# The next item's turn behind both halves of gate and up, and the routing tables written late, in an adaLN attention and expert block on one core

## The chip, the cores and the metric

The kernel runs on one core of a Trainium2 chip. The metric is the device time of one execution in microseconds (us), lower is better. The core has five engines with an instruction stream each: TensorE (PE, with its weight loads as PEld), VectorE (DVE), ScalarE (ACT), GpSimd (POOL) and SyncE (SP). Each works through its stream in order; they meet only at semaphores, which one engine raises and another waits for.

## The reference

For 4 sequences of 512 tokens of width 256 the reference computes an adaLN block: modulation rows from a condition, attention, and a mixture of experts.

```python
h = _layernorm(x) * (1 + ca) + sa
x = x + ga * attention(h)          # 16 heads of 16, 4 key/value heads
h = _layernorm(x) * (1 + cb) + sb
probs = softmax(h @ router_w.T)    # 8 experts
w = _top_p_weights(probs, 0.9)     # keep the likeliest experts up to 0.9
for e in range(8):
    g = silu(h @ gate_w[e].T)      # 256 -> 512
    u = h @ up_w[e].T
    out = out + ((g * u) @ down_w[e].T) * w[:, e:e+1]
x = x + gb * out
```

All of it is in f32. The expert products are made of three matmuls each: an operand is rounded to a high part (ScalarE) and its rest becomes a low part (VectorE), and high times high, high times low and low times high are added.

## The kernel before, in words

**Start.** SP loads the condition, the first sequence and the weights. VectorE computes the means and variances of sequence 0 and GpSimd takes the power (L337). VectorE then writes `xhat` (L660), which TensorE turns (L1102) and projects to queries, keys and values. Meanwhile GpSimd writes constants, one after another (L339 to L353): zeros and ones, two masks (`tie`, `earlier`), `ones_b`, the ones of `v_aug`, and four tables by iota (`slot_row`, `slot_tile`, `token1`, `pad_row`). Each raises `consts`; GpSimd waits for all eight, then for the variances of sequences 1 to 3, takes their power (L357), and issues four DMAs that write zeros to `y_rows` and to the end of `h_rows`. VectorE and TensorE both wait for all of `consts` before attention. Of these constants attention reads only the ones of `v_aug`; the rest is for routing.

**Attention** runs sequence by sequence. While the scores, exponentials and products of sequence b run, the engines also prepare sequence b + 1 and finish b - 1. Then come the routing and the lists of tokens for each expert.

**Experts.** The tokens of each expert are cut into items of 256 (two tiles of 128 rows). In this input there are 25 items in all. In the loop over items each engine runs one body for item m, and the bodies are written out by hand:

- GpSimd gathers the rows of a later item into `h_sel` (L391, two indirect DMAs). It does so when the turn of the item before has read `h_sel` (`turned`) and VectorE has copied that item's weights from it (`w_copied`). It then scatters the outputs of an earlier item with addition (L404, two indirect DMAs).
- TensorE: gate and up for the first half of the hidden width (`gate_up(m, half, 0)`, L1340, 24 matmuls), the turn of item m + 1 (`turn`, L1326, 4 transposes), gate and up for the second half (24 matmuls), then down of item m - 1 in two halves (`down`, L1353, 12 matmuls each, one after the other). The next item's first matmul waits for `sel_lo`.
- ScalarE: silu of the first half (`gate`, L557); once both halves of item m are done, the high part of the next input (`round_input`, L552, writes `hs_hi`); then the high part of the first hidden half (`round_hidden`, L562, writes `a_hi`), silu of the second half, and its high part.
- VectorE: copy of the next item's weights (`take_weights`, L1014), product of the first half (`product`, L1020, writes `a_full`), low part of the next input (`split_input`, L1008, writes `hs_lo`, raises `sel_lo`), low part of the first hidden half (`split_hidden`, L1025, writes `a_lo`), product of the second half, output of item m - 1 (`output`, L1035, writes `y_sel`), low part of the second hidden half.

`hs_hi`, `hs_lo`, `h_sel` and `psM` exist once. `a_hi` and `a_lo` exist once for each half, and are read by `down`. Hence the wait in ScalarE's `round_hidden`, with `FREE = 2` and `down_ps` raised by 2 at the start and by 1 for each half of down:

```python
act.wait_ge(a_ready, 2 * m + h + 1 + FREE)
act.wait_ge(down_ps, 2 * m + h - 1 + FREE)
```

After the first item of an expert ScalarE rounds the next expert's weights and VectorE splits them (`between_experts`). The loop over experts is a loop over four pairs, and every engine jumps back three times.

Of the kernel before, what the change touches and what calls it, by code (L numbers as in the profile page):

```python
# [21 lines left out]
P = 128  # L22
# [8 lines left out]
def adaln_block(nc, x, wqT, wkT, wvT, woT, routerT, gateT, upT, downT, cT, wmod, out):  # L31
# [29 lines left out]
    with ctx:  # L61
# [14 lines left out]
        def sems(names):  # L76
            return [sem(n) for n in names.split()]
# [78 lines left out]
        for parts, part in ((w_hi, "w_hi"), (w_lo, "w_lo")):  # L156
# [43 lines left out]
        zeroed, ident_done, consts, silu_step, modc_ps, modc_done, modr_ps, row_copied, mod_out, mod_in, gate_step, modr_done = sems(  # L200
            "zeroed ident_done consts silu_step modc_ps modc_done modr_ps row_copied mod_out mod_in gate_step modr_done")
# [25 lines left out]
        NCONST = 8  # L227
# [98 lines left out]
        def _(pool):  # L326
# [11 lines left out]
            for m, v in ((v_aug[:, :, :, :, D:YROWS], 0.0), (tie[:, :, :], 1.0), (earlier[:, :], 1.0), (zeros[:, :], 0.0)):  # L338
                pool.memset(m, v).then_inc(zeroed, 1)  # L339
# [6 lines left out]
            pool.memset(v_aug[:, :, :, :, D:D + 1], 1.0).then_inc(consts, 1)  # L346
# [5 lines left out]

# [3 lines left out]
            pool.wait_ge(ln1_eps, 2)  # L356
            pool.tensor_tensor(rstd1[:, TT:], var_eps1[:, TT:], minus_half[:, 0:NT - TT], ALU.pow).then_inc(ln1_rstd, 1)  # L357

            for r0, r1 in ((0, T // 2), (T // 2, T), (T, T + PADS)):
                pool.dma_start(y_rows[r0:r1, :].rearrange("(t p) c -> p t c", p=P),  # L360
                               zeros[:, 0:C].rearrange("p (o c) -> p o c", o=1).broadcast_to([P, (r1 - r0) // P, C])
                               ).then_inc(scattered, 16)
            pool.dma_start(h_rows[T:T + PADS, :].rearrange("(t p) c -> p t c", p=P),
                           zeros[:, :].rearrange("p (o c) -> p o c", o=1).broadcast_to([P, S, ROW])).then_inc(scattered, 16)
# [66 lines left out]
        def _(act):  # L431
# [132 lines left out]
            def body(e, e2, first, m, half):  # L564
                gate(m, 0)
                act.wait_ge(up_ps, 2 * m + 2)
                round_input(m + 1)
                round_hidden(m, 0)
                gate(m, 1)
                round_hidden(m, 1)  # L570
# [17 lines left out]
        def _(dve):  # L588
# [319 lines left out]
            dve.wait_ge(consts, NCONST)  # L908
            attention(dve, body)
            take_sums(B - 1, G - 1)  # L910
            finish_y(B - 1, (B - 1) % 2, G - 1)
            choose_experts(0)
# [99 lines left out]

# [27 lines left out]
            def body(e, e2, first, m, half):  # L1040
                take_weights(m + 1)
                product(m, 0)
# [356 lines left out]
```

## Time and profile before

| | us |
|---|---|
| median of 3 runs | 614.0 (613.22 to 616.6) |
| the profiled execution, its own time | 614.37 |
| span of its profile | 612.6 |
| TensorE busy | 483.4 (79% of the span) |
| VectorE busy | 371.3 (61%) |
| ScalarE busy | 282.5 (46%) |
| GpSimd busy | 170.9 (28%) |

The span starts with the first instruction and ends with the last. Times in rows are microseconds from its start; the mean granted TensorE clock is 0.894 of full speed. The rest of the execution's own time (1.8 us) lies outside the span.

### The profile page before, as it was taken

What the parts mean: (1) busy time and instruction counts of PE and PEld (TensorE: products, weight loads), DVE (VectorE), ACT (ScalarE), POOL (GpSimd) and SP (SyncE); (2) the same over time, 40 slices, a digit from 0 to 9 for tenths busy, and PEclk for the clock granted to TensorE, in tenths of its full rate; (3) what the DMA queues carried; (4) which work ended last, traced back from release to release, by engine and by line L of the source; (5) the groups of instructions that cost most, each with busy time, mean ns of one, the idle gap of its engine ahead of it and who ended that gap; (6) DMA issues with size and microseconds to landing.
All of it is one profiled execution on the core that took longest, in us unless ns stands there. A gap on an engine that the chain in (4) does not pass through costs nothing. (4 is left out here: it accounts for less than half of the span.)

```text
span 612.6 us, 10534 instructions
## 1 busy us (share of the span) xinstructions
PE 483.4 (79%) x3498; PEld 351.2 (57%) x3499; DVE 371.3 (61%) x910; ACT 282.5 (46%) x409; POOL 170.9 (28%) x184
## 2 busy tenths in 40 slices
PE   2745978898899789997315599999997998999810
PEld 2333323244344433425215599999997998999810
DVE  4496287669936983567678175665643755465526
ACT  0244669776886788782000244453423543443300
POOL 6104000000000000000000336656665556476440
PEclk9965989998999999987655699999998998999975
DMA  8243100000000010010121134636453446333338
GB/s 291 95 135 117 61 1 1 1 0 2 24 13 1 1 35 1 1 35 1 34 73 35 46 104 98 158 60 164 90 125 61 109 98 151 56 52 60 44 37 271
DMA packets 33815, 42.01 MB, mean 69 GB/s; under 512 B 5620, under 2 KB 26868, under 8 KB 33784
## 3 DMA queue, kind: packets, MB, share of 16 engines
q0 software_dynamic: 10400, 16.22, 14.5%
q1 hardware_dynamic: 23384, 25.39, 13.0%
q8 instruction: 18, 0.29, 0.2%
q14 instruction: 13, 0.11, 0.1%
HBM read 28.14 MB, written 13.46 MB: 68 GB/s over the span
## 5 line engine op out<-in xcount | busy, mean ns | idle before, releaser
L511 ACT ACTIVATE probs<-psS 128x1024 f32<-128x1024 f32 x128 | 124.0, 1023 | 16.3 <-PE psS L1162 16.0
L1340 PE MATMUL psS<-hs_hi,w_hi 128*128 128x256 f32 x400 | 117.5, 294 | 6.9 <-issue 3.9
L1340 PE MATMUL psS<-hs_lo,w_hi 128*128 128x256 f32 x400 | 114.4, 286 | 0.0
L1340 PE MATMUL psS<-hs_hi,w_lo 128*128 128x256 f32 x400 | 114.3, 286 | 0.0
L404 POOL DMA_INDIRECT y_rows<-y_sel,idx_out x50 | 83.4, 1668 | 55.3 <-DVE y_sel L1035 45.0
L1340 PEld LDWEIGHTS psS<-hs_hi,w_hi 128*128 128x128 f32 x400 | 77.5, 194 | 8.4 <-issue 7.7
L1162 PE MATMUL psS<-qT,kT 96*128 96x512 bf16 x256 | 71.7, 393 | 11.1 <-ACT probs L511 9.4
L1340 PEld LDWEIGHTS psS<-hs_lo,w_hi 128*128 128x128 f32 x400 | 77.7, 194 | 0.0
L1340 PEld LDWEIGHTS psS<-hs_hi,w_lo 128*128 128x128 f32 x400 | 77.5, 194 | 0.0
L1271 PE MATMUL psY<-probs,v_aug 128*32 128x512 f32 x512 | 70.8, 626 | 0.0
L369 POOL TENSOR_TENSOR rstd<-var_eps,minus_half 128x4 f32<-128x4 f32 x4 | 4.8, 1195 | 235.2 <-DVE var_eps L764 235.2
L552 ACT CAST hs_hi<-psM 128x512 fp32r<-128x512 f32 x26 | 15.3, 587 | 117.0 <-PE psS L1340 76.7
L391 POOL DMA_INDIRECT h_sel<-h_rows,idx_in x50 | 52.9, 1058 | 38.6 <-issue 20.3
L1353 PE MATMUL psY<-w_hi,a_hi 128*128 128x256 f32 x200 | 56.1, 280 | 1.6 <-DVE y_sel L1035 1.6
L1353 PE MATMUL psY<-w_lo,a_hi 128*128 128x256 f32 x200 | 56.0, 280 | 0.0
L1353 PE MATMUL psY<-w_hi,a_lo 128*128 128x256 f32 x200 | 56.0, 280 | 0.0
L1008 DVE TENSOR_TENSOR hs_lo<-psM,hs_hi 128x512 fp32r<-128x512 f32 x26 | 18.0, 692 | 59.5 <-ACT hs_hi L552 51.5
L562 ACT CAST a_hi<-a_full 128x512 fp32r<-128x512 f32 x50 | 31.1, 621 | 42.7 <-PE psY L1353 23.2
L1162 PEld LDWEIGHTS psS<-qT,kT 96*128 96x128 bf16 x256 | 21.5, 99 | 46.9 <-ACT probs L511 29.9
L1025 DVE TENSOR_TENSOR a_lo<-a_full,a_hi 128x512 fp32r<-128x512 f32 x50 | 34.6, 692 | 20.1 <-ACT a_hi L562 16.1
L1353 PEld LDWEIGHTS psY<-w_hi,a_hi 128*128 128x128 f32 x200 | 37.6, 188 | 1.8 <-issue 1.8
L1353 PEld LDWEIGHTS psY<-w_hi,a_lo 128*128 128x128 f32 x200 | 37.6, 188 | 0.0
(188 smaller groups left out, 807.6 us busy)
## 6 DMA issues: line engine op xcount, KB each, us to landing
w_in<-gateT SPq DMA_DIRECT2D x8, 512.0 KB
w_in<-upT SPq DMA_DIRECT2D x8, 512.0 KB
w_in<-downT SPq DMA_DIRECT2D x8, 512.0 KB
x_all<-x SPq DMA_DIRECT2D x4, 512.0 KB, 7.9
mod_rows<-mod_table SPq DMA_DIRECT2D x4, 512.0 KB, 7.6
y_rows<-zeros POOLq DMA_DIRECT2D x2, 1024.0 KB
h_rows<-h_nat SPq DMA_DIRECT2D x4, 512.0 KB, 3.0
y_all<-y_rows SPq DMA_DIRECT2D x4, 512.0 KB, 5.7
```

Of the source, the lines that this page charges most:

```text
L369: pool.tensor_tensor(rstd[:, :], var_eps[:, :], minus_half[:, 0:TT], ALU.pow).then_inc(ln_rstd, 1)
L391: pool.indirect_dma_start(h_sel[:, k, :], None, h_rows[:, :], bass.IndirectOffsetOnAxis(ap=idx_in[:, k:k + 1], axis=0)).then_inc(gathered, 16)
L404: pool.indirect_dma_start(y_rows[:, :], bass.IndirectOffsetOnAxis(ap=idx_out[:, k:k + 1], axis=0), y_sel[:, k, :], None, compute_op=ALU.ad ...
L511: act.activation(probs[:, gk % 4, 2 * pair:2 * pair + 2, :], psS[:, pair, :, :], ACT.Exp, scale=ATT_SCALE).then_inc(probs_done, 1)
L552: act.copy(hs_hi[:, :, :].rearrange("p k t -> p (k t)"), psM[:, 0, :]).then_inc(sel_hi, 1)
L562: act.copy(a_hi[:, 2 * h:2 * h + 2, :].rearrange("p i t -> p (i t)"), a_full[:, h, :]).then_inc(a_rounded, 1)
L1008: dve.tensor_tensor(hs_lo[:, :, :].rearrange("p k t -> p (k t)"), psM[:, 0, :], hs_hi[:, :, :].rearrange("p k t -> p (k t)").bitcast(F32), ...
L1025: dve.tensor_tensor(a_lo[:, 2 * h:2 * h + 2, :].rearrange("p i t -> p (i t)"), a_full[:, h, :], a_hi[:, 2 * h:2 * h + 2, :].rearrange("p i ...
L1162: mm = pe.matmul(psS[:, u % 2, j, :], kT[:, parity, g, kt * P:(kt + 1) * P], qT[:, parity, g * R + 2 * pair + j, :], start=True, stop=True)
L1271: mm = pe.matmul(psY[r * YROWS:(r + 1) * YROWS, g % 2, :], v_aug[:, parity, kt, g, :], probs[:, gk % 4, r, :], start=kt == 0, stop=kt == T ...
L1340: mm = pe.matmul(ps[:, i * SW:(i + 1) * SW], w, v[:, k, :], start=at == 0, stop=at == 3 * KC - 1)
L1353: mm = pe.matmul(psY[:, j, 0:C], v[:, i, tok], w, start=i == 0 and n == 0, stop=i == KI - 1 and n == 2)
```

## The change

In the expert loop the turn of item m + 1 moves behind both halves of gate and up. ScalarE's body becomes: silu of the first half, high part of the first hidden half, silu of the second half, high part of the next input, high part of the second hidden half. VectorE's body becomes: product and low part of the first half, the copy of the next item's weights, product of the second half, low part of the next input, low part of the second hidden half, output of item m - 1. No wait inside these helpers changes.

At the start GpSimd writes only `v_aug` (its ones raise a semaphore of their own, `v_ones`), then waits for the variances of sequences 1 to 3, takes their power, writes `zeros` and issues the four DMAs; after them come the masks and the four tables. TensorE waits for `v_ones` before the first score, and for `consts` before the ranks; VectorE waits for `consts` before it chooses experts.

```diff
             pool.wait_ge(ln1_eps, 1)
             pool.tensor_tensor(rstd1[:, 0:TT], var_eps1[:, 0:TT], minus_half[:, 0:TT], ALU.pow).then_inc(ln1_rstd, 1)
-            for m, v in ((v_aug[:, :, :, :, D:YROWS], 0.0), (tie[:, :, :], 1.0), (earlier[:, :], 1.0), (zeros[:, :], 0.0)):
-                pool.memset(m, v).then_inc(zeroed, 1)
+
+            pool.memset(v_aug[:, :, :, :, D:YROWS], 0.0).then_inc(zeroed, 1)
+            pool.wait_ge(zeroed, 4)
+            pool.memset(v_aug[:, :, :, :, D:D + 1], 1.0).then_inc(v_ones, 1)
+            pool.wait_ge(ln1_eps, 2)
+            pool.tensor_tensor(rstd1[:, TT:], var_eps1[:, TT:], minus_half[:, 0:NT - TT], ALU.pow).then_inc(ln1_rstd, 1)
+
+            pool.memset(zeros[:, :], 0.0).then_inc(zeroed, 1)
+            pool.wait_ge(zeroed, 5)
+            for r0, r1 in ((0, T // 2), (T // 2, T), (T, T + PADS)):
+                pool.dma_start(y_rows[r0:r1, :].rearrange("(t p) c -> p t c", p=P),
+                               zeros[:, 0:C].rearrange("p (o c) -> p o c", o=1).broadcast_to([P, (r1 - r0) // P, C])
+                               ).then_inc(scattered, 16)
+            pool.dma_start(h_rows[T:T + PADS, :].rearrange("(t p) c -> p t c", p=P),
+                           zeros[:, :].rearrange("p (o c) -> p o c", o=1).broadcast_to([P, S, ROW])).then_inc(scattered, 16)
+
+            for m in (tie, earlier):
+                pool.memset(m[:, :], 1.0).then_inc(zeroed, 1)
             pool.wait_ge(zeroed, 7)
             pool.affine_select(out=tie[:, :, :], in_=tie[:, :, :], compare_op=ALU.is_gt, fill=0.0, base=0,
                                pattern=[[1, E], [-1, E]], channel_multiplier=0).then_inc(consts, 1)
             pool.affine_select(out=earlier[:, :], in_=earlier[:, :], compare_op=ALU.is_gt, fill=0.0, base=0,
                                pattern=[[1, P]], channel_multiplier=-1).then_inc(consts, 1)
             pool.memset(ones_b[:, :], 1.0).then_inc(consts, 1)
-            pool.memset(v_aug[:, :, :, :, D:D + 1], 1.0).then_inc(consts, 1)
             small = dict(allow_small_or_imprecise_dtypes=True)
             pool.iota(slot_row[:, :, :], [[1, P], [0, NT]], base=0, channel_multiplier=0, **small).then_inc(consts, 1)
             pool.iota(slot_tile[:, :, :, :], [[1, TSLOTS], [0, NT], [0, E]], base=0, channel_multiplier=0,
                       **small).then_inc(consts, 1)
             pool.iota(token1[:, :, :], [[P, NT], [0, E]], base=1, channel_multiplier=1, **small).then_inc(consts, 1)
-
             pool.iota(pad_row[:, :, :, :], [[0, E], [0, TSLOTS // 2], [P, 2]], base=T + 1, channel_multiplier=1,
                       **small).then_inc(consts, 1)
             pool.wait_ge(consts, NCONST)
-            pool.wait_ge(ln1_eps, 2)
-            pool.tensor_tensor(rstd1[:, TT:], var_eps1[:, TT:], minus_half[:, 0:NT - TT], ALU.pow).then_inc(ln1_rstd, 1)
-
-            for r0, r1 in ((0, T // 2), (T // 2, T), (T, T + PADS)):
-                pool.dma_start(y_rows[r0:r1, :].rearrange("(t p) c -> p t c", p=P),
-                               zeros[:, 0:C].rearrange("p (o c) -> p o c", o=1).broadcast_to([P, (r1 - r0) // P, C])
-                               ).then_inc(scattered, 16)
-            pool.dma_start(h_rows[T:T + PADS, :].rearrange("(t p) c -> p t c", p=P),
-                           zeros[:, :].rearrange("p (o c) -> p o c", o=1).broadcast_to([P, S, ROW])).then_inc(scattered, 16)
 
...
             def body(e, e2, first, m, half):
                 gate(m, 0)
+                round_hidden(m, 0)
+                gate(m, 1)
                 act.wait_ge(up_ps, 2 * m + 2)
                 round_input(m + 1)
-                round_hidden(m, 0)
-                gate(m, 1)
                 round_hidden(m, 1)
...
-            dve.wait_ge(consts, NCONST)
             attention(dve, body)
             take_sums(B - 1, G - 1)
             finish_y(B - 1, (B - 1) % 2, G - 1)
+            dve.wait_ge(consts, NCONST)
             choose_experts(0)
...
             def body(e, e2, first, m, half):
+                product(m, 0)
+                split_hidden(m, 0)
                 take_weights(m + 1)
-                product(m, 0)
+                product(m, 1)
                 split_input(m + 1)
-                split_hidden(m, 0)
-                product(m, 1)
+                split_hidden(m, 1)
                 if first and half == 0:
                     with dve.If(e2 > 0):
                         output(e, m - 1)
                 else:
                     output(e if first else e + 1, m - 1)
-                split_hidden(m, 1)
...
-            pe.wait_ge(consts, NCONST)
+            pe.wait_ge(v_ones, 1)
             score(0, 0, 0)
...
             pe.wait_ge(rt_kept, 4)
+            pe.wait_ge(consts, NCONST)
...
                 pe.wait_ge(sel_lo, m + 1)
                 gate_up(m, half, 0)
+                gate_up(m, half, 1)
                 turn(m + 1)
-                gate_up(m, half, 1)
```

## Rows read from the trace of the kernel before

**Rows 1.** Chain that ended last, 512 to 535 us: start, us, what.
```profile
512.59 4.21 DMA h_sel<-h_rows,idx_in
...
517.53 4.33 PE psS L1340 x24
...
528.01 0.44 PE psM L1326 x4
528.45 2.83 PE psS L1340 x24
```

**Rows 2.** TensorE's waits, 340 to 582 us: total, times, longest.
```profile
PE psM L1326 <- DMA h_sel<-h_rows,idx_in: 10.7, 2, 8.6
PE psS L1340 <- issue: 3.9, 3, 3.2
```

**Rows 3.** Timeline of GpSimd, 0 to 62 us: start, us, instruction.
```profile
9.95 2.48 POOL L348 IOTA slot_row<- 128x2048 f16 x1
...
16.54 0.96 POOL L353 IOTA pad_row<- 128x128 f32 x1
52.04 2.28 POOL L357 TENSOR_TENSOR rstd<-var_eps,minus_half 128x12 f32<-128x12 f32 x1 [34.54 <-DVE var_eps L617]
54.26 3.48 POOL L360 DMA_DIRECT2D y_rows<-zeros  x3
```

**Rows 4.** Timeline of VectorE, 0 to 62 us.
```profile
10.51 7.13 DVE L660 TENSOR_SCALAR xhat<-x_all,mean_var,rstd 128x256 f32<-128x256 f32 x4
...
56.54 1.37 DVE L660 TENSOR_SCALAR xhat<-x_all,mean_var,rstd 128x256 f32<-128x256 f32 x4
```

**Rows 5.** Timeline of VectorE, from 55 us.
```profile
70.73 0.56 DVE L667 TENSOR_TENSOR squares<-qkv 128x384 f32<-128x384 f32 x1 [12.82 <-ACT qkv L461]
```

**Rows 6.** Timeline of TensorE, 0 to 62 us.
```profile
17.79 1.94 PE L1102 MATMUL psM<-ident,xhat 128*128 128x128 f32 x8 [7.67 <-DVE xhat L660]
```

**Rows 7.** ScalarE's waits, 352 to 582 us: total, times, longest.
```profile
ACT a_hi L562 <- PE psY L1353: 23.2, 28, 0.9
```

**Rows 8.** Timeline of TensorE, last item, 572 to 585 us.
```profile
576.27 0.28 PE L1353 MATMUL psY<-w_hi,a_hi 128*128 128x256 f32 x1
...
580.88 0.36 PE L1353 MATMUL psY<-w_hi,a_hi 128*128 128x256 f32 x1 [1.63 <-DVE y_sel L1035]
```

**Rows 9.** Timeline of ScalarE in the same item.
```profile
576.55 0.59 ACT L552 CAST hs_hi<-psM 128x512 fp32r<-128x512 f32 x1 [4.36 <-PE psS L1340]
577.94 0.62 ACT L562 CAST a_hi<-a_full 128x512 fp32r<-128x512 f32 x1 [0.80 <-PE psY L1353]
578.46 0.59 ACT L557 ACTIVATE silu_g<-psS 128x512 f32<-128x512 f32 x1
579.99 0.62 ACT L562 CAST a_hi<-a_full 128x512 fp32r<-128x512 f32 x1 [0.93 <-DVE a_full L1020]
```

**Rows 10.** Timeline of VectorE in the same item.
```profile
577.17 0.69 DVE L1008 TENSOR_TENSOR hs_lo<-psM,hs_hi 128x512 fp32r<-128x512 f32 x1 [3.19 <-ACT hs_hi L552]
578.66 0.69 DVE L1025 TENSOR_TENSOR a_lo<-a_full,a_hi 128x512 fp32r<-128x512 f32 x1 [0.80 <-ACT a_hi L562]
579.27 0.68 DVE L1020 TENSOR_TENSOR a_full<-psS,silu_g 128x512 f32<-128x512 f32 x1
579.87 0.87 DVE L1035 TENSOR_SCALAR y_sel<-psY,w_sel 128x256 f32<-128x256 f32 x2
```

**Rows 11.** VectorE's copy of the weights, in the timeline from 336 us.
```profile
358.85 0.17 DVE L1014 TENSOR_SCALAR w_sel<-h_sel 128x16 f32 x1
```

**Rows 12.** GpSimd's gather behind it, in the timeline from 336 us.
```profile
359.83 0.97 POOL L391 DMA_INDIRECT h_sel<-h_rows,idx_in  x1 [6.18 <-DVE w_sel L1014]
```

**Rows 13.** VectorE between items 0 and 1, from 340 us.
```profile
351.91 0.69 DVE L1008 TENSOR_TENSOR hs_lo<-psM,hs_hi 128x512 fp32r<-128x512 f32 x1 [3.27 <-issue]
```

**Rows 14.** TensorE at the same place.
```profile
352.73 0.38 PE L1340 MATMUL psS<-hs_hi,w_hi 128*128 128x256 f32 x1 [1.55 <-DVE hs_lo L1008]
```

**Rows 15.** Busy time by stretch: stretch, length, PE, PEld, DVE, ACT, POOL, granted clock, DMA share, GB/s.
```profile
353.00:380.00 27.00, 27.00 (x230) 26.90 (x230) 15.65 (x27) 11.52 (x18) 12.89 (x15) 1.00 0.44 102
```

More of the change, by code:

```diff
@@ L198, in adaln_block @@
         y_in = [sem(f"y_in{b}") for b in range(B)]
-        zeroed, ident_done, consts, silu_step, modc_ps, modc_done, modr_ps, row_copied, mod_out, mod_in, gate_step, modr_done = sems(
-            "zeroed ident_done consts silu_step modc_ps modc_done modr_ps row_copied mod_out mod_in gate_step modr_done")
+        zeroed, ident_done, v_ones, consts, silu_step, modc_ps, modc_done, modr_ps, row_copied, mod_out, mod_in, gate_step, modr_done = sems(
+            "zeroed ident_done v_ones consts silu_step modc_ps modc_done modr_ps row_copied mod_out mod_in gate_step modr_done")
         (bn1_done, ln1_stats, ln1_eps, ln1_rstd, mods_done, xhat_done, xT_ps, hT_done, qkv_ps, qkv_sb, squared, sq_sum,
@@ L226, in adaln_block @@
         ROUTE_STEPS = 12
-        NCONST = 8
+        NCONST = 7
         FREE = 2
```

## The prediction, made before the changed kernel ran

> **What bounds the kernel now.** I read the chain that ended last, then TensorE's waits, then the timelines of each engine, in two places: the start and the expert loop.
>
> In the expert loop TensorE is the bound. The chain there is a row of TensorE groups with nothing between them: 24 matmuls of the first half (2.83 us), 4 transposes (spaced 0.36 to 0.44), 24 of the second half and 24 of down, of the same shape and length [rows 1]. That is 8.9 us for an item. Between 340 and 582 us TensorE waited hardly at all. The longest stalls are the first gather (8.6), one late gather (10.7 - 8.6 = 2.1) and three stalls put down to nothing but issue, 3.9 in total, of which one is 3.2 [rows 2]. I take these three for the three jumps back of the loop over pairs of experts, because that is their number. The other engines have slack, and so the question is whether the new orders keep it.
>
> At the start the bound is a chain of small steps, and one of them is odd. VectorE's four `xhat` instructions took 7.13 us for sequence 0 and 1.37 us, same form, for sequence 1 [rows 4]. The first set ran from 10.5 to 17.6 us, beside GpSimd's iotas, which ran from 9.95 to 17.5 [rows 3]. TensorE sat idle for 7.67 us until `xhat` was there [rows 6].
>
> **The start, step by step.** The tables move behind the second power, so `xhat` of sequence 0 runs alone and should take 1.37 instead of 7.13: 5.8 us less, on a path where TensorE was waiting for it. The Trainium skill ("SBUF - State Buffer", section "Who interferes with whom") has GpSimd and VectorE share a port pair under an exclusive lock and the loser block for the whole instruction. The trace agrees (7.13 against 1.37 us), and by that rule the tables cost the same again if VectorE has such work beside them.
>
> The rows say where they land. The second power began at 52.04 and took 2.28 [rows 3]; 5.8 earlier, it ends near 48.5. GpSimd then issues the DMAs, 3.5 for three of the four, so I take some 5 with the fourth and the zeros. The iotas are 7.5 long [rows 3] and the masks perhaps 1, so these run from about 53.5 to 62. VectorE finishes `xhat` of sequence 1 near 52 and then waits for sequence 1's projections: it was idle for 12.8 us until 70.73 before [rows 5], which becomes 52 to 65. Its idle time hides the tables; if it did not, up to 5.8 would come back. The tables have no reader before routing near 300 us. The `v_ones` wait is met near 9 us. Everything in attention hangs on that start, so I carry all of it: **-5.8**.
>
> **The loop, step by step.** Moving the turn itself costs TensorE nothing: the same four transposes. The next input's high and low parts could still hide under down. But ScalarE's new order puts `round_hidden(m, 0)` before `gate(m, 1)` and `round_input(m + 1)`, and that instruction waits for `down_ps >= 2m + 1`. With the 2 given at the start, this is the first half of down of item m - 1: `a_hi` exists once, and down reads it. Down of m - 1 stands in TensorE's stream after both halves of gate and up of item m. The trace shows the wait bite: 28 times ScalarE waited for TensorE's down before `a_hi`, 0.8 us each [rows 7]. In the old order the next input had already gone past. Now it is queued behind.
>
> Let t be the first down matmul of an item (576.27 in the last one) [rows 8]. The spacing of the old rows gives the new sequence:
>
> - `a_hi` of the first half starts at t + 1.67, silu of the second half at t + 2.19 [rows 9]. The next activation follows 0.5 later, so `hs_hi` starts near t + 2.7. It started at t + 0.3 before.
> - VectorE: `a_lo` at t + 2.39 and the next instruction 0.6 later [rows 10], so `w_sel` at t + 3.0, which takes 0.1 to 0.2 [rows 11]. The product of the second half then starts at t + 3.1; its silu allows it (t + 2.19 plus 0.8). `hs_lo` follows 0.6 later, at t + 3.7; by `hs_hi` alone it could have started at t + 3.3 (0.62 behind it [rows 9, 10]).
> - TensorE restarts 0.82 after `hs_lo` starts [rows 13, 14]: t + 4.5. Down ends at t + 2.83. The stall is 1.7 us.
>
> Bounds: 1.3 if VectorE were never in the way (t + 3.3 + 0.82), 2.1 if its instructions beside GpSimd are 0.2 longer twice.
>
> It falls between item m and m + 1 for m = 1 to 23. Item 0 has no down in its body, and its old stall of 1.55 [rows 14] stays: the turn is on that path, and equally much has left the matmuls ahead of it. At the three jumps the stall overlaps with the one that is there: two grow from 0.35 to 1.7, the one of 3.2 hides it. So 20 x 1.7 + 2 x 1.35 = **+36.7**.
>
> The late gather goes. A turn now needs its rows 2.8 us later in the item. The gather itself also waits for the weights' copy, now at t + 3.0: it starts 0.98 behind that, its second part some 1.3 later (the first is 0.97 long) [rows 11, 12], and lands 4.2 after that [rows 1], at t + 9.5. The next turn comes at t + 4.5 + 2 x 2.83 = t + 10.2. With 0.7 us of slack at the slowest landing seen there is no stall. This returns the 2.1 of waiting, 1.5 of slow clock behind it (24 matmuls in 4.33 instead of 2.83 [rows 1]) and 0.2 on the transposes: **-3.8**. The scatter starts behind that gather, near t + 7.7, and the output of the next item needs it only a period (10.6) plus 5.1 after t, so it hides. Rounding and splitting the next expert's weights stays behind the bodies of ScalarE and VectorE; it delays silu and product of the next item's first half, whose reader `a_hi` waits for TensorE's down anyway.
>
> The tail: the last down and the last scatters wait for the output of item 23, which started at t + 3.6 [rows 10]. In the new order the second `a_hi` starts 0.72 behind its product [rows 9, 10], t + 3.8; `a_lo` 0.7 later, t + 4.5; output at t + 5.1. **+1.5**.
>
> **Sum**, against the profiled execution's own 614.37: - 5.8 + 36.7 - 3.8 + 1.5 = + 28.6, which is 643.0. The median of the runs lies 0.4 below that execution, so 642.6.
>
> **Rivals.**
>
> 1. *The clock falls behind the new stalls.* Behind the idle time of 2.1 us the matmuls ran 1.5 us slow: that is the lower of the two levels, 1.2 instead of 2.4 GHz. Behind idle times of 1.55 and 1.63 they did not (granted 1.00 from 353 us on) [rows 1, 8, 14, 15]. The new stalls of 1.7 lie next to the harmless ones. If half of the 23 cost 1.5, the time is 660; all of them, 677. The Trainium skill ("TensorE: Matmul & The Clock Gate", section "A second HAM failure mode: psum-queue depth-cycling") warns of this: short idle gaps between groups of matmuls, repeated, make the clock fall and rise. It would give the 660 to 677. No repeated gap of this kind stands in the trace. Chance 0.17.
> 2. *The turn only gains slack; the loop keeps its 8.9 us (ends on the other side).* Then only the start and the late gather count: 614.0 - 5.8 - 3.8 = 604.4. It decides if ScalarE's high part does not wait for down, or if the wait is met before silu of the second half would run. Against it stands the count of 28 [rows 7] and the arithmetic of the semaphore. It would take a stall under 0.4 us to turn the sign. Chance 0.05.
> 3. *The gathers come late.* They now start some 3 us later against the turn before. If each landed 1 us later than the slowest one seen, the stall would grow by 0.3 on 20 items: 649. For it: tables, weights and scatters share the queues. Against it: 0.7 us of slack. Chance 0.08.
> 4. *The start gives nothing* (the 7.13 us had another cause, or attention loses it to the tables): 648.4. Against it stands the end of `xhat` 0.1 us behind the end of the iotas. Chance 0.08.
>
> The forecast itself has 0.62. With 20 stalls between 1.3 and 2.1 its own range is 634 to 651. Rivals 3 and 4 lie in it; from rival 1 the cases with few slow stalls, up to ten of the 23, reach 658. So the range is 634 to 658. A measurement of this kernel tells no less than about 0.5% (3 us) from no change. Faster by more than that has 0.04 and within it 0.01, both from rival 2 (a small stall can just make up for the gains); slower has 0.95.
>
> **What the profile after would show.** Right: TensorE waiting for `hs_lo` over 20 times, 1.7 each; `hs_hi` starting behind silu of the second half, some 2.7 us behind the first down matmul; an item of 10.6 us; matmuls of one length throughout the loop; `xhat` of sequence 0 in 1.4 us and the first turn near 12 us; tables between 54 and 62 us beside an idle VectorE. Wrong: no wait for `hs_lo`; a stretch of the loop at half clock; waits for the gather on TensorE; VectorE's instructions longer near 55 us.

## The result, and the profile after

| | before | after |
|---|---|---|
| median of 4 runs each, us | 614.75 (613.22 to 616.6) | 644.44 (641.08 to 645.86) |
| the profiled execution, its own time | 614.37 | 643.14 |
| span of its profile | 612.6 | 641.4 |
| mean granted clock | 0.894 | 0.899 |

The changed kernel takes 1.0475 times as long (95% interval 1.0438 to 1.0512). The prediction said 642.6, with a range of 634 to 658.

The work is the same. Part 1 of the page of after has TensorE 3 us busier than before (483.4) and the span 29 us longer, so what was added is waiting.

```profile
PE 486.2 (76%) x3498; PEld 351.8 (55%) x3499; DVE 361.6 (56%) x910; ACT 279.7 (44%) x409; POOL 170.6 (27%) x184
```

The waits of TensorE in the loop of after (334 to 612 us: total, times, longest) stand where [rows 2] stand for before.

```profile
PE psS L1345 <- DVE hs_lo L1013: 36.1, 24, 1.5
PE psM L1331 <- DMA h_sel<-h_rows,idx_in: 8.6, 1, 8.6
PE psY L1358 <- DVE y_sel L1039: 3.2, 1, 3.2
PE psS L1345 <- issue: 3.2, 1, 3.2
```

Behind each item, TensorE now waits for the low part of the next input, `hs_lo`; before, it did so twice (3.1 us), before the first item and behind it. The second gather wait (2.1) is gone. Of the three issue stalls only the long one is left to see; the two short ones lie inside the new wait.

Here is one passage from an item to the next in the timelines of after. TensorE first. Its first down matmul, t of the prediction, is at 428.65, and it is back at gate and up at 433.23.

```profile
428.30 0.60 PE L1331 MATMUL psM<-ident,h_sel 128*128 128x128 f32 x4
428.65 0.37 PE L1358 MATMUL psY<-w_hi,a_hi 128*128 128x256 f32 x1
...
433.23 0.38 PE L1345 MATMUL psS<-hs_hi,w_hi 128*128 128x256 f32 x1 [1.51 <-DVE hs_lo L1013]
```

ScalarE in the same passage.

```profile
430.40 0.62 ACT L567 CAST a_hi<-a_full 128x512 fp32r<-128x512 f32 x1 [5.57 <-PE psY L1358]
430.93 0.59 ACT L562 ACTIVATE silu_g<-psS 128x512 f32<-128x512 f32 x1
431.42 0.58 ACT L557 CAST hs_hi<-psM 128x512 fp32r<-128x512 f32 x1
432.53 0.62 ACT L567 CAST a_hi<-a_full 128x512 fp32r<-128x512 f32 x1 [0.53 <-DVE a_full L1024]
```

VectorE in the same passage.

```profile
431.12 0.69 DVE L1029 TENSOR_TENSOR a_lo<-a_full,a_hi 128x512 fp32r<-128x512 f32 x1 [4.78 <-ACT a_hi L567]
431.74 0.17 DVE L1018 TENSOR_SCALAR w_sel<-h_sel 128x16 f32 x1
431.81 0.68 DVE L1024 TENSOR_TENSOR a_full<-psS,silu_g 128x512 f32<-128x512 f32 x1
432.41 0.68 DVE L1013 TENSOR_TENSOR hs_lo<-psM,hs_hi 128x512 fp32r<-128x512 f32 x1
433.25 0.69 DVE L1029 TENSOR_TENSOR a_lo<-a_full,a_hi 128x512 fp32r<-128x512 f32 x1 [0.15 <-ACT a_hi L567]
433.86 0.87 DVE L1039 TENSOR_SCALAR y_sel<-psY,w_sel 128x256 f32<-128x256 f32 x2
```

The input of the next item has been in `psM` since 429. ScalarE could have rounded it at once, but its next instruction is the rounding of the first hidden half. That one sat for 5.57 us until TensorE's down had read the old `a_hi`, and everything for the next item stands behind it. Before, `hs_hi` came 0.3 us after the first down matmul and ahead of that wait [rows 8, 9].

The start moved the other way. These are the first instructions of GpSimd (memsets, then the second power, the DMAs, the tables), in the timeline of after; compare [rows 3].

```profile
8.17 0.52 POOL L339 MEMSET v_aug<- 128x512 f32 x1
...
46.30 2.27 POOL L343 TENSOR_TENSOR rstd<-var_eps,minus_half 128x12 f32<-128x12 f32 x1 [37.40 <-DVE var_eps L622]
49.15 2.78 POOL L348 DMA_DIRECT2D y_rows<-zeros  x3 [0.32 <-POOL zeros L345]
53.69 2.48 POOL L363 IOTA slot_row<- 128x2048 f16 x1
56.12 3.81 POOL L364 IOTA slot_tile<- 128x2048 f16 x1
60.15 1.01 POOL L367 IOTA pad_row<- 128x128 f32 x1
```

And VectorE over the same time, to set beside [rows 4, 5].

```profile
10.52 1.38 DVE L665 TENSOR_SCALAR xhat<-x_all,mean_var,rstd 128x256 f32<-128x256 f32 x4
...
50.70 1.67 DVE L665 TENSOR_SCALAR xhat<-x_all,mean_var,rstd 128x256 f32<-128x256 f32 x4
65.04 0.56 DVE L672 TENSOR_TENSOR squares<-qkv 128x384 f32<-128x384 f32 x1 [12.67 <-ACT qkv L466]
```

Without a table beside it `xhat` of sequence 0 takes 1.38 instead of 7.13 us, and TensorE begins at 12.04 instead of 17.79 [rows 6]. The tables now run from 53.7 to 61.2, while VectorE stands idle until 65.04.

```profile
12.04 1.94 PE L1106 MATMUL psM<-ident,xhat 128*128 128x128 f32 x8 [1.91 <-DVE xhat L665]
```

### The profile page after: what moved, and what is told of

It reads as the page before. It is cut to its first block, busy times and chain, and to the rows that moved or that the text cites. A ratio compares the mean times of both kernels' runs of the same rounds, so it can differ in the third digit from the quotient of the medians.

```text
span 641.4 us, 10535 instructions
## 1 busy us (share of the span) xinstructions
PE 486.2 (76%) x3498; PEld 351.8 (55%) x3499; DVE 361.6 (56%) x910; ACT 279.7 (44%) x409; POOL 170.6 (27%) x184
## 4 chain that ended last, share of the span: by engine, by line
issue 41%; PE 34%; DVE 14%; ACT 3%; DMA 3%; POOL 3%; ACTq 0%; DVEq 0%; POOLq 0%; SPq 0%
PE psS L1345 24%; PE psY L1358 5%; DVE hs_lo L1013 2%; ACT silu_g L562 2%; DVE a_full L1024 2%; PE psM L1331 2%; PE psM L1118 1%; DMA y_rows<-y_sel,idx_out 1%; DVE one_row L969 1%; DVE y_all L1078 1%; DVE y_all L1076 1%; DMA w_mod<-wmod 1%; DVE w_sel L1018 1%; DMA y_all<-y_rows 1%; DVE stats L616 1%
## 5 line engine op out<-in xcount | busy, mean ns | idle before, releaser
L1345 PE MATMUL psS<-hs_hi,w_hi 128*128 128x256 f32 x400 | 116.3, 291 | 39.3 <-DVE hs_lo L1013 36.1
L396 POOL DMA_INDIRECT h_sel<-h_rows,idx_in x50 | 50.3, 1006 | 98.8 <-DVE w_sel L1018 83.9
L1358 PE MATMUL psY<-w_hi,a_hi 128*128 128x256 f32 x200 | 58.1, 291 | 3.2 <-DVE y_sel L1039 3.2
L1024 DVE TENSOR_TENSOR a_full<-psS,silu_g 128x512 f32<-128x512 f32 x50 | 34.3, 686 | 36.2 <-PE psS L1345 32.9
L1166 PEld LDWEIGHTS psS<-qT,kT 96*128 96x128 bf16 x256 | 21.5, 99 | 46.8 <-ACT probs L516 29.7
L562 ACT ACTIVATE silu_g<-psS 128x512 f32<-128x512 f32 x50 | 29.7, 594 | 26.9 <-PE psS L1345 26.8
L1358 PEld LDWEIGHTS psY<-w_lo,a_hi 128*128 128x128 f32 x200 | 37.7, 189 | 0.0
```

Source lines behind the costliest of these rows:

```text
L396: pool.indirect_dma_start(h_sel[:, k, :], None, h_rows[:, :], bass.IndirectOffsetOnAxis(ap=idx_in[:, k:k + 1], axis=0)).then_inc(gathered, 16)
L562: act.activation(silu_g[:, h, :], psS[:, 0, h, :], ACT.Silu).then_inc(silu_ready, 1)
L1024: dve.tensor_tensor(a_full[:, h, :], psS[:, 1, h, :], silu_g[:, h, :], ALU.mult).then_inc(a_ready, 1)
L1166: mm = pe.matmul(psS[:, u % 2, j, :], kT[:, parity, g, kt * P:(kt + 1) * P], qT[:, parity, g * R + 2 * pair + j, :], start=True, stop=True)
L1345: mm = pe.matmul(ps[:, i * SW:(i + 1) * SW], w, v[:, k, :], start=at == 0, stop=at == 3 * KC - 1)
L1358: mm = pe.matmul(psY[:, j, 0:C], v[:, i, tok], w, start=i == 0 and n == 0, stop=i == KI - 1 and n == 2)
```

## The experiments

Each kernel is an edit of the changed kernel unless the text says otherwise, and its time stands beside that of the kernel before on the same chip. The change itself was not run again beside them. The medians of the kernel before lie between 613.5 and 615.4 us in these comparisons, so a difference from the change's 644.4 can be off by some 2 us. None leaves work out. The first two were made to split the change, the next four (e3 to e6) to find which position costs the time, e7 and e8 to double a suspected cost, and the last four to see what the late turn itself is worth.

### e1: the start alone

The start of after, the loop orders of before on all three engines (the diff of the loop, undone).

> The start alone, with the loop of before. Theory (the tables blocked VectorE's xhat, and the whole gain is carried to the end): xhat of sequence 0 in 1.4 us, experts' first turn 5.3 us earlier than before, the loop at 8.9 us an item, time 5.3 to 5.8 below before: about 609. Rival (the gain is eaten later, or the loop is disturbed by the shift): 612 or more.

Measured: 608.37 against 614.73, ratio 0.989 (0.981 to 0.997). The start alone gives 6.4 us, with an interval from 2.1 to 11.6. In the loop the old waits are back, here TensorE's.

```profile
PE psM L1331 <- DMA h_sel<-h_rows,idx_in: 10.7, 2, 8.5
PE psS L1345 <- issue: 3.8, 3, 3.2
PE psS L1345 <- DVE hs_lo L1013: 3.1, 2, 1.6
```

### e2: the loop alone

The start of before, the loop of after.

> The loop's new order alone, with the start of before. Theory (the two parts add): TensorE waits about 1.5 us for hs_lo at 20 or more items, an item takes 10.7 us, and the time is that of the whole change plus 5.3 to 5.8: about 650. Rival (the longer item comes from the tables' or DMAs' new place, or the parts overlap): below 645.

Measured: 650.41 against 614.73, ratio 1.056 (1.050 to 1.063). The loop alone costs 35.7 us, and TensorE waits for `hs_lo` 24 times again, 36.1 in total. The parts add up: -6.4 + 35.7 = +29.3, where the whole change gives +29.7 (644.44 - 614.75). Within the width of these intervals, some 5 us, no interplay of the two parts is seen.

### e3: the next input ahead of the hidden halves

The turn stays late. ScalarE and VectorE split the next input before they touch a hidden half:

```diff
 (ScalarE)
                 gate(m, 0)
-                round_hidden(m, 0)
                 gate(m, 1)
                 act.wait_ge(up_ps, 2 * m + 2)
                 round_input(m + 1)
+                round_hidden(m, 0)
                 round_hidden(m, 1)
 (VectorE)
                 product(m, 0)
-                split_hidden(m, 0)
                 take_weights(m + 1)
                 product(m, 1)
                 split_input(m + 1)
+                split_hidden(m, 0)
                 split_hidden(m, 1)
```

Each product also waits until the low part of the item before has been made from the same half of `a_full` (`a_split`), since that no longer follows from the order. This wait belongs to the edit.

> The whole change, but ScalarE and VectorE do the next input before the first hidden half: ScalarE silu 0, silu 1, hs_hi, a_hi 0, a_hi 1; VectorE product 0, weights, product 1, hs_lo, a_lo 0, a_lo 1, output; one more wait (a_split) in the product. TensorE's late turn stays. Theory (hs_hi is queued behind an a_hi that waits for down): hs_hi about 0.3 us behind the first down matmul, hs_lo ready 1.7 behind it, under down's 2.8; no wait for hs_lo except behind item 0; before minus the start's 5.3 and the late gather's 3.8: about 605.5. Rival (the late turn itself cannot be hidden under down): the stalls stay, 635 or more.

Measured: 605.72 against 614.73, ratio 0.983 (0.978 to 0.988): 39 us faster than the change, by the order of a few instructions alone. Two of the 24 waits for `hs_lo` are left in TensorE's list.

```profile
PE psM L1332 <- DMA h_sel<-h_rows,idx_in: 8.6, 1, 8.6
PE psS L1346 <- issue: 4.0, 3, 3.2
PE psS L1346 <- DVE hs_lo L1013: 3.0, 2, 1.5
```

ScalarE's timeline of e3 has the same wait for down as after, but now behind `hs_hi`, where nothing that TensorE needs next is queued. The first down matmul of this item is at 444.10, so `hs_hi` is back at t + 0.3.

```profile
444.38 0.58 ACT L557 CAST hs_hi<-psM 128x512 fp32r<-128x512 f32 x1 [1.26 <-PE psM L1332]
445.87 0.62 ACT L567 CAST a_hi<-a_full 128x512 fp32r<-128x512 f32 x1 [0.90 <-PE psY L1359]
```

### e4: the low part of the input right behind the first hidden half

```diff
 (VectorE)
                 product(m, 0)
                 split_hidden(m, 0)
+                split_input(m + 1)
                 take_weights(m + 1)
                 product(m, 1)
-                split_input(m + 1)
```

> The whole change, but VectorE does hs_lo straight behind a_lo of the first half, ahead of the weights' copy and the second product. Theory (ScalarE's hs_hi at 2.7 us behind the first down matmul is the floor, VectorE adds the rest): hs_lo starts at 3.3 instead of 3.5 us behind it, so each stall shrinks by 0.2 us, 20 times: some 4 us under the whole change, about 640. Rival (VectorE's order is the cause): stalls vanish, about 606. Other rival (ScalarE alone counts): the same time as the whole change.

Measured: 636.82 against 614.73, ratio 1.033 (1.028 to 1.039). One stall of the loop, in TensorE's timeline:

```profile
433.92 0.38 PE L1345 MATMUL psS<-hs_hi,w_hi 128*128 128x256 f32 x1 [1.12 <-DVE hs_lo L1013]
```

It is 0.4 shorter than the 1.51 of after, twice what was expected: the expectation put `hs_lo` of after too early, and it stands at t + 3.76 (432.41 - 428.65). The copy of the weights and the second product, which stand ahead of `hs_lo` in after, account for these 0.4 us. What is left does not belong to one engine: in this passage of e4 VectorE's `a_lo`, still ahead of `hs_lo`, ends at 432.89 and ScalarE's `hs_hi` at 433.07, and both stand behind the `a_hi` that waits for down.

### e5: ScalarE's order mended, VectorE's left

> The whole change, with only ScalarE's order mended (silu 0, silu 1, hs_hi, a_hi 0, a_hi 1); VectorE still does a_lo of the first half ahead of hs_lo. Theory (whichever engine puts the down wait ahead of the next input, the stall is the same, since VectorE's a_lo needs the a_hi that waits for down): hs_hi some 0.3 to 0.6 us behind the first down matmul, but a_lo 2.4 and hs_lo 3.5 behind it as before; TensorE's wait stays 1.5 an item; about 644. Rival (ScalarE's order is the whole cause): about 606.

```diff
 (ScalarE)
                 gate(m, 0)
-                round_hidden(m, 0)
                 gate(m, 1)
                 act.wait_ge(up_ps, 2 * m + 2)
                 round_input(m + 1)
+                round_hidden(m, 0)
                 round_hidden(m, 1)
```

Measured: 647.71 against 614.29, ratio 1.055 (1.051 to 1.060), no better than the change. ScalarE's high part is on time, 0.3 us after the first down matmul (433.37); the row is of ScalarE's timeline.

```profile
433.65 0.59 ACT L557 CAST hs_hi<-psM 128x512 fp32r<-128x512 f32 x1 [1.26 <-PE psM L1331]
```

But on VectorE the low part of the hidden half still stands first, and waits for the `a_hi` that waits for down.

```profile
435.86 0.69 DVE L1029 TENSOR_TENSOR a_lo<-a_full,a_hi 128x512 fp32r<-128x512 f32 x1 [4.79 <-ACT a_hi L567]
...
437.14 0.68 DVE L1013 TENSOR_TENSOR hs_lo<-psM,hs_hi 128x512 fp32r<-128x512 f32 x1
```

So the same wait is placed at the head of two queues, and mending ScalarE's alone gives nothing: `hs_lo` is at t + 3.77 in e5 and t + 3.76 in after. Mending VectorE's alone was not run. The profiled execution of e5 is 6.1 us longer than that of after (the medians differ by 3.3). One stall behind item 0 is 1.9 longer (3.34 us), the 48 matmuls behind it take 8.55 instead of 5.94, and the 48 behind the 3.2 us stall at a jump take 8.63 instead of 7.46. Why that one stall is longer stays open.

### e6: down of the old item split around the second half

ScalarE and VectorE as in the change; TensorE gives the first half of down earlier, so that the wait of `a_hi` is met earlier. (`earlier_down(h)` is the call of `down` for item m - 1 as it stood, one half at a time.)

```diff
 (TensorE)
                 gate_up(m, half, 0)
+                earlier_down(0)
                 gate_up(m, half, 1)
                 turn(m + 1)
-                (both halves of down of item m - 1)
+                earlier_down(1)
```

> The whole change with all orders of ScalarE and VectorE kept, but TensorE does the first half of down of item m - 1 between the two halves of gate and up, so that the awaited semaphore comes some 3 us earlier. Theory (the wait for down is the cause): a_hi 0 runs under the second half of gate and up; the turn, hs_hi and hs_lo then lie under 1.4 us of down only and take about 0.3 + 0.6 + 0.8 = 1.7 us, so 0.3 us of stall an item are left; 7 us over the mended version's 606: 610 to 615. Rival (the order of the engines itself or the late turn costs the time, whatever down does): 640 or more.

Measured: 611.14 against 614.29 over 10 runs, ratio 0.996 (0.993 to 0.999). This is the strongest test of the cause: no instruction moved on ScalarE or VectorE, only what `a_hi` waits for comes earlier, and TensorE's waits for `hs_lo` fall from 24 (36.1 us) to 5 (3.8 us). This is TensorE's list of waits in e6:

```profile
PE psS L1345 <- DVE hs_lo L1013: 3.8, 5, 1.5
```

Two of the five are those before and behind item 0. The 0.3 us an item that was expected is there all the same, mostly as gaps too short for the list: an item of e6 takes 9.30 us (411.64 to 420.94) against 9.03 on average before. Over 22 items that is 5.9 us, about the 5.4 between the medians of e6 and e3.

### e7: one table back at the start

```diff
 (GpSimd)
             pool.memset(v_aug[:, :, :, :, D:D + 1], 1.0).then_inc(v_ones, 1)
+            pool.iota(slot_tile[:, :, :, :], [[1, TSLOTS], [0, NT], [0, E]], base=0, channel_multiplier=0, ...)
             pool.wait_ge(ln1_eps, 2)
...
-            pool.iota(slot_tile[:, :, :, :], [[1, TSLOTS], [0, NT], [0, E]], base=0, channel_multiplier=0, ...)
```

> The whole change, but the table slot_tile is written at its old place near 9 us, right behind the ones of v_aug; the others stay late. Theory (VectorE's copies stand still while an iota runs): with an iota of 3.8 us from about 8.9 to 12.7, the copy of mods and the first xhat wait for its end, xhat ends near 14 instead of 11.9, and the first turn starts some 2.2 us later than in the whole change. Rival (the start's gain comes from the waits on the constants that were split): xhat ends at 11.9 as in the whole change.

It ran once: 647.25, span 645.5, so its total time is not compared; its rows are. GpSimd's timeline of e7 has the table here:

```profile
8.73 3.82 POOL L342 IOTA slot_tile<- 128x2048 f16 x1
```

VectorE's timeline of e7 beside it:

```profile
10.05 0.24 DVE L799 TENSOR_SCALAR mod_cols<-psM 128x8 f32<-128x8 f32 x2 [3.08 <-PE psM L1090]
10.32 2.25 DVE L662 COPY mods<-mod_cols 128x4 f32<-128x4 f32 x1
10.40 3.27 DVE L665 TENSOR_SCALAR xhat<-x_all,mean_var,rstd 128x256 f32<-128x256 f32 x4
```

And TensorE's:

```profile
13.81 1.94 PE L1106 MATMUL psM<-ident,xhat 128*128 128x128 f32 x8 [3.80 <-DVE xhat L665]
```

In after the copy `mods`, four elements a partition, takes 0.17 us. Beside the iota it takes 2.25, until 12.57, and the iota ends at 12.55. TensorE starts 1.8 us later than in after (12.04) and sat idle for 3.80 instead of 1.91 us. The table holds `mods` and `xhat` until it ends, and that is the cause of the 7.13 us before. It does not hold everything on VectorE: the first row, `mod_cols`, which reads `psM`, ran in the middle of the same table and took 0.24 us, as long as in after without one.

### e8: the low part of the input last

```diff
 (VectorE)
                 product(m, 1)
-                split_input(m + 1)
                 split_hidden(m, 1)
+                split_input(m + 1)
```

> The whole change, but VectorE does hs_lo behind a_lo of the second half. The stall of each item grows by some 0.8 us (hs_lo at 4.3 instead of 3.5 us behind the first down matmul), to 2.3. Theory (stalls add up one for one): 20 x 0.8 = 17 us over the whole change, about 661. Rival (the clock falls behind idle times over 2 us, as it did once before behind 2.1): up to 1.5 us more for each of some 20 items, 670 to 690, and stretches of the loop at a granted clock under 1.00.

Measured: 710.89 against 614.29, ratio 1.161 (1.155 to 1.167): 66 us more than the change, for one VectorE instruction moved behind another. TensorE's list of waits in e8:

```profile
PE psS L1345 <- DVE hs_lo L1013: 72.4, 25, 3.2
```

One of these waits in TensorE's timeline:

```profile
457.50 0.58 PE L1345 MATMUL psS<-hs_hi,w_hi 128*128 128x256 f32 x1 [2.97 <-DVE hs_lo L1013]
```

The expectation of 0.8 more per stall was wrong by its size: the second `a_hi` and its `a_lo` come first, at t + 3.9 and t + 4.6, so `hs_lo` is at t + 5.2 (456.68, with the first down matmul at 451.47) and the stall is 1.45 longer. That explains half. The chain that ended last shows the other half (start, us, what): the 48 matmuls behind the stall take 7.42 us.

```profile
457.50 7.42 PE psS L1345 x48
```

In after the same piece of the chain is this:

```profile
433.23 5.95 PE psS L1345 x48
```

So 1.5 us a stall are lost to the lower clock level, 1.2 instead of 2.4 GHz, which lasts about 3 us. An item takes 10.71 + 1.45 + 1.49 = 13.65. The view of busy time by stretch (columns as in [rows 15]) says the same. The granted clock is 0.89 in this stretch of e8:

```profile
440.00:470.00 30.00, 22.26 (x160) 21.67 (x158) 9.95 (x20) 7.80 (x15) 12.06 (x13) 0.89 0.29 62
```

In after it is 1.00:

```profile
440.00:470.00 30.00, 25.49 (x212) 24.90 (x211) 15.74 (x27) 11.17 (x18) 15.89 (x16) 1.00 0.45 101
```

### e9 to e12: what the late turn is worth

e3 left open whether its gain over e1 (605.7 against 608.4) has anything to do with the late turn. e9 is e3 with the turn between the halves again; e10 is e3 with VectorE's output ahead of the second low part; e11 is e10 with the early turn; e12 is e11 with the copy of the weights first. e3's gain over e1 is small beside their intervals, which overlap.

```diff
 (e9 and e11, TensorE)
                 gate_up(m, half, 0)
-                gate_up(m, half, 1)
                 turn(m + 1)
+                gate_up(m, half, 1)
 (e10, VectorE)
                 split_hidden(m, 0)
-                split_hidden(m, 1)
                 output(...)
+                split_hidden(m, 1)
 (e12, VectorE, on top of e11)
+                take_weights(m + 1)
                 product(m, 0)
-                take_weights(m + 1)
```

> The mended version (next input ahead of the first hidden half on ScalarE and VectorE, start of the whole change) with the turn back between the two halves of gate and up. Theory (the late turn gives only the slack for a late gather): TensorE waits once more for a gather, about 2.1 us plus 1.5 us at the lower clock, so 3 to 4 us over the mended version's 605.7: about 609, like the start alone. Rival (the late turn has no part, the mended order alone removed the late gather): 605.7.

> The mended version with VectorE's output of item m - 1 ahead of a_lo of the second half. Theory (the end hangs on the last outputs alone, the loop on TensorE): the output of item 23 starts some 0.8 us earlier and so does the end; 605 against 605.7, within what can be told. Rival (an output that waits for the scatter holds up a_lo and with it down): some us slower.

> The early turn with the mended order, and VectorE's output of item m - 1 ahead of a_lo of the second half (some 3.6 us behind the first down matmul, as in the kernel before, instead of 4.4). Theory (in the run with the early turn the later output made the scatters late, and the gathers queued behind them on GpSimd came late for the turn): with the output back in its place the gather waits fall from eight to two or three, and the time to 606 to 610. Rival (the order of ScalarE or the weights' copy behind the first product makes the gathers late): seven or eight gather waits stay, 618 or more.

> This is the kernel with the early turn and the earlier output (615.8), with the copy of the weights put ahead of the first product on VectorE, as the kernel before has it. Theory: the gathers are late because GpSimd may issue one only when the weights are copied, and behind the first product that copy comes late. Then the seven gather waits of 0.2 to 2.5 us (9 in total) and the slow clock behind the longer ones go, but for one of about 2: 604 to 607 us. Rival: the gathers are late because with an early turn there is no slack at all between the second gather's landing (some 3.3 us behind its issue) and the turn, wherever the copy stands, and any later step of GpSimd's ring shows: 612 to 618 us, with five or more waits.

| | turn | us | before, same chip | ratio (95%) | TensorE's gather waits behind the first, us |
|---|---|---|---|---|---|
| e3 | late | 605.72 | 614.73 | 0.983 (0.978 to 0.988) | none |
| e9 | early | 619.56 | 613.46 | 1.012 (1.004 to 1.020) | 9.7, 7 times |
| e10 | late | 603.63 | 613.46 | 0.982 (0.976 to 0.987) | none |
| e11 | early | 615.75 | 615.37 | 1.000 (0.997 to 1.003) | 8.9, 7 times |
| e12 | early | 614.85 | 614.54 | 1.001 (0.999 to 1.003) | 7.5, 7 times |

e9 was expected at 609 and is a miss. With the mended orders the turn's place is worth 12 to 14 us between the medians (e9 against e3, e11 against e10), or 10 to 15 if each is first set against the kernel before on its own chip. Put early, the turn waits for its gather seven times more. That is the price of an early turn in the new orders; beside e1, an early turn in the old ones, the late turn of e3 and e10 gains only 3 to 5 us. TensorE's list of waits of e12:

```profile
PE psM L1332 <- DMA h_sel<-h_rows,idx_in: 16.0, 8, 8.5
```

One such wait in its timeline:

```profile
418.06 0.66 PE L1332 MATMUL psM<-ident,h_sel 128*128 128x128 f32 x4 [1.49 <-DMA h_sel<-h_rows,idx_in]
```

The gather's second part had been issued at 413.49, so it landed 4.6 us later (GpSimd's timeline of e12):

```profile
413.49 1.29 POOL L396 DMA_INDIRECT h_sel<-h_rows,idx_in  x1 [0.30 <-issue]
```

In e10, with the late turn, a gather has mostly 4 to 6 us until the turn (6.1 for the one issued at 427.31 and turned at 433.41), and the turn does not wait.

Two theories of why the gathers are late fell. It is not the late output (e11 was expected near 606 to 610 by that), and not the copy of the weights behind the first product (e12, expected 604 to 607 by that, measured 614.85). The time and the count of waits came out as e12's rival had them, but its reason, that an early turn leaves the gather no slack, is only half the story. e1 has the early turn too, and there 3.25 us (issue at 429.34, turn at 432.59) were enough, with one wait of 2.15 us as the exception. In e12 two things are worse for the gathers that the turn waited for. They were issued only 1.5 to 3.1 us before TensorE was ready for the turn, in e1 mostly 2.9 to 3.7. And they were used 2.8 to 4.6 us behind their issue, so some of them also landed later than 3.25. Why they do, though both kernels issue the same transfers, no run settles: the DMA traffic around the four latest is high (183 to 225 GB/s), but in e1 gathers beside 210 GB/s and more came in time. Nor was ScalarE's new order run by itself with an early turn.

## Why the prediction was right, point by point

- **The cause.** `a_hi` waits for down of the old item, and the next input is queued behind it. Right: the wait is at the place that was named, and e3, e5 and e6 show it from three sides (input ahead of the wait on both engines: gone; on ScalarE alone: not gone; the wait met earlier with nothing moved on either engine: all but gone). The prediction named ScalarE's queue as the place and treated VectorE's as a follower. e5 shows that VectorE's is a full second one.
- **The stall's size.** Forecast: `hs_lo` at t + 3.7, TensorE back at t + 4.5, stall 1.7. Measured: `hs_lo` at t + 3.76, back at t + 4.58 (433.23 - 428.65). The item went to 10.71 us. Before, it was not the 8.9 that the prediction read from one place, but 9.03 on average over the 19 items without a jump or the late gather (8.92 to 9.18), so it grew by 1.68. The two readings, 8.9 before and 10.6 after, were both about 0.1 low, and the difference between them was right. The timeline shows 1.51 of the stall as idle, since it counts from 431.72, t + 3.07, the modelled end of the last down matmul, where the prediction counted from t + 2.83.
- **The loop's sum.** From the first gate and up to the first down matmul of the last item it was 576.27 - 343.31 = 232.96 before and is 603.23 - 338.00 = 265.23: +32.3. Forecast: +36.7 - 3.8 = +32.9. Term by term: the two items with a short jump stall grew by 1.1 and 1.3 (forecast 1.35 each), the one with the 3.2 us stall did not grow (13.95 before, 13.90 after), and the rest is the 1.68 of every other item less the late gather.
- **The late gather.** Gone; there is one gather wait in after, the first. The turn comes 4.9 us behind the issue of the gather's second part, 0.7 more than the 4.2 of the slowest landing seen before, as the sum had it. e9 to e12 add what the prediction could not see: with the new orders an early turn would wait seven times more.
- **The start.** Forecast -5.8. In the profile TensorE's first turn is 5.75 earlier, the first turn of the experts 5.31 (340.69 to 335.38): in this pair attention gave 0.4 back. How closely that agrees is partly luck. In the eleven profiles with the new start unaltered (after and all but e2 and e7) the experts' first turn came anywhere from 333.37 to 337.77, 4.4 us apart, and e1 has -6.4 in the medians, with an interval from 2.1 to 11.6. e7 shows the mechanism. The Trainium skill ("SBUF - State Buffer", section "Who interferes with whom") has the loser of the shared port pair block for the whole instruction of the other; in e7 a copy of four elements a partition stood until 0.02 us behind the end of the iota, so the trace agrees for that copy.
- **The tables' new place.** Forecast 53.5 to 62 beside an idle VectorE; they ran from 53.7 to 61.2, and VectorE was idle from 52.4 to 65.04. The one thing not forecast: `xhat` of sequence 1 took 1.67 instead of 1.37. The cause is open, since GpSimd issued the same DMAs beside it before. The next step, `squares`, came 5.69 us earlier, so little of it shows.
- **The tail.** Forecast +1.5. Output of item 23 started at t + 5.21 (608.44) instead of t + 3.60, +1.6, and the rest to the end took 0.2 more (32.96 against 32.73).
- **The sum.** -5.3 + 32.3 + 1.6 + 0.2 = +28.8, the difference of the spans (641.4 - 612.6). Forecast +28.6. Errors of both signs cancel in it (0.5 less gained at the start, 0.6 less lost in the loop, 0.3 more lost at the end), so that it agrees to 0.2 us is luck.
- **The clock, the main rival.** It did not fall behind the new stalls: granted 1.00 through the loop, but for the first item behind the 8.6 us gather wait and for the item behind the 3.2 us stall at a jump (48 matmuls in 7.46 instead of 5.94 us), which before had too. The doubt was right to price, though. e8 shows what it costs: with idle times of 2.95, repeated, each stall is followed by some 3 us at half speed, and that alone costs some 1.5 us a time. The Trainium skill ("TensorE: Matmul & The Clock Gate", section "A second HAM failure mode: psum-queue depth-cycling") warns of short gaps, frequently repeated. The gaps of 1.51 us in after did not do what it describes, and those of 2.95 in e8 did.
- **The other-sided rival** (the turn only gains slack, 604.4) is not what this change does, but nearly what e3 and e10 do: with the order mended, 605.7 and 603.6.

## What to carry to other kernels

When an instruction moves in a hand-written order, look up what it waits for and then read what stands behind it in the same queue: here the work did not grow, and one wait on a single-buffered tile (`a_hi`) moved ahead of the next item's input cost 1.7 us an item. Such a wait must be mended in every queue that holds it: mending ScalarE's alone (e5) gave nothing, and both together (e3) gave 39 us. And a step that gives a transfer more slack is only worth its gain if the engines that read behind it keep their order: late turn plus input first, with the output ahead of the second low part (e10), is the best version run here, 603.63 us, 1.8% faster than the kernel before (1.3 to 2.4).

## What the runs showed of the hardware beyond the forecast

- Idle times of up to 1.83 us on TensorE were followed by matmuls at full speed in every kernel run here: 23 of about 1.5 in after, 1.63 before, 1.64 in e11, 1.83 in e12. (One of 1.53, before the first item, follows the 8.6 us gather wait, and the matmuls are slow there in every kernel.) The 24 idle times of 2.67 to 3.21 in the loop of e8 were each followed by slow ones (48 matmuls in 7.3 to 7.4 instead of 5.95 us).
- Above that the length alone does not decide. The clock fell behind 2.16 (before), 2.15 (e1), 1.98 (e9) and 2.51 (e11), and stayed at 1.00 behind 1.99 and 2.18 (e9), 2.05 (e11) and 2.44 (e12). Behind the last wait for `y_sel` the 12 matmuls of down ran at full speed in after and e2 (3.18) and at half speed in e5 and e7 (3.16). Here are the shorter and the longer one of e9 in TensorE's timeline:

```profile
387.88 0.75 PE L1332 MATMUL psM<-ident,h_sel 128*128 128x128 f32 x4 [1.98 <-DMA h_sel<-h_rows,idx_in]
...
519.90 0.66 PE L1332 MATMUL psM<-ident,h_sel 128*128 128x128 f32 x4 [2.18 <-DMA h_sel<-h_rows,idx_in]
```

And the stretches of e9 that hold them (columns as in [rows 15]; the matmuls behind the second one begin at 520.3), with granted clocks of 0.94 and 1.00:

```profile
370.00:400.00 30.00, 27.58 (x219) 27.10 (x218) 15.79 (x26) 12.91 (x19) 17.33 (x18) 0.94 0.50 107
520.00:550.00 30.00, 29.40 (x245) 28.80 (x246) 16.39 (x28) 13.10 (x19) 18.59 (x20) 1.00 0.37 71
```

- The price of a fall is not fixed either: the 48 matmuls behind it took 1.5 us longer behind the 2.95 of e8, and 2.6 and 2.7 longer behind 3.34 and 3.16 in e5.
- An iota on GpSimd held VectorE's copy `mods` and its `xhat` until it ended, however small the work: a copy of 128x4 took 2.25 us instead of 0.17. It did not hold a VectorE instruction that reads `psM` (0.24 us beside it and without it).
- From the issue of a gather's second part to its use by the turn, 3.25 us were enough in e1. In e12 the gathers that the turn waited for took 2.8 to 4.6.
- A stall of 3.2 us on TensorE at one of the loop's three jumps is in the lists of before, after, e1 and e3. Where an item also waits for `hs_lo`, the two do not add up: the shorter lies inside the longer (3.2 in all in after). In e8, with stalls of 2.95, the item at that jump waited 3.21.
